# Softmax sums of a windowed attention: two key blocks added on GpSimd, and the ones matmuls moved behind the row's next product

## The chip, the cores and the metric

One NeuronCore of a Trainium2 chip runs the whole program. The metric is the device time of one execution in microseconds.

## The reference

Eight parts run one after the other on 4096 tokens of 128 features: a gated linear recurrence, a two-layer transformer with windowed attention, an attention with ALiBi biases, a mixture of experts, an attention with 8-wide rotated heads, a feed-forward net with ternary weights, a low-rank attention with 32-wide rotation, and a linear layer given in the frequency domain. The change touches the windowed attention alone. It is called for two layers, over 16 rows of 256 tokens, with 8 heads of 64 features:

```python
def local_attention(q, k, v):            # window w = 64 tokens
    bq = q.reshape(b, h, w, WINDOW, d) * QK_SCALE
    ...                                  # each query block looks at its own key block and the one before
    sim = jnp.einsum('bhwid,bhwjd->bhwij', bq, bk)
    mask = (i < j) | (i > j + WINDOW) | (j == -1)
    sim = jnp.where(mask, -jnp.finfo(sim.dtype).max, sim)
    attn = jax.nn.softmax(sim, axis=-1)
    out = jnp.einsum('bhwij,bhwjd->bhwid', attn, bv)
```

The softmax's denominator is, for each query, the sum of its weights over the keys of two blocks (of one block for the first query block).

## The kernel before

`local_attention` (L974) writes a separate program for each engine. `every_row` (L953) walks i over 16 rows plus a tail of 5, and each `step` is cut into four quarters x = 0 to 3. A quarter works on several rows at once: it projects row i (`product`, L1064), transposes row i-1 or i-2 (`columns_of`, L1072), takes scores of row i-2 or i-3 for the maxima (`scores`, L1090), and for row i-4 computes the exponentiated weights (`keyed`, L1104, then ScalarE L1244) and the attention itself (`values`, L1126). The heads come in two groups g; group 0 is attended in quarter 1 and group 1 in quarter 3. The output projection (`output`, L1152) of row i-5 stands in quarter 1. "A full row" below is a step with i from 5 to 15, in which every one of these is alive: 11 in each layer.

The order on each engine is the order of the code. Semaphores tie the engines together, and PSUM banks limit them: bank 0 holds the product, banks 2 and 3 the attention's values (columns 0 to L) and its sums (L to 2L), and bank 1 is used twice in every quarter, once by `columns_of` and once by a second job: project_values (L1144) in quarters 0 and 3, output in 1, shifts (L1158) in 2. `ends` and `bank_read` (L1167 to L1183) make either user wait until the one before was read. So `columns_of` in quarter 2 waits until row i-5's output was added to the residual and stored, which is L1376 on VectorE; in quarters 0, 1 and 3 it waits for a copy by ScalarE.

TensorE's order in quarter 1 is columns_of, values of group 0, output, product; in quarter 3 columns_of, values of group 1, project_values, product. `values` holds, for each of four key blocks j, four 64x64 matmuls with V and four with ones, over 128 query columns (64 for the last block). They read the weights `pr`, laid out by key block: for query block j the weights of its two key blocks stand beside one another, 64 columns each, after the lone first 64 columns.

After the ones matmuls come, per group: on ScalarE the logarithm (`lsum`, L1247) and an exponential (`rec`, L1250), on VectorE `near_one` (L1290, instruction L1294), on ScalarE `left` (L1276), on GpSimd `inv` (L1047), on VectorE `divide` (L1296, instruction L1301), which frees banks 2 and 3. VectorE's order in quarters 1 and 3 is `near_one`, then (quarter 1) L1376, then `rotate` (L1338). In quarter 0 it is `clamped` (L1322), divide of group 1, `maximum`, `inverse_norms` (L1328, its last instruction L1335), `negated` (its last L1320), rotate. GpSimd's order in a quarter is `qn` (L1039), in quarters 1 and 3 `inv`, then `tc` (L1052), and in quarter 2 two shifted copies (L1026, L1028). ScalarE's quarter ends with the square of the product (`sq`, L1272) and `left`.

Of the kernel before, what the change touches and what calls it, by code (L numbers as in the profile page):

```python
# [12 lines left out]
ALU = mybir.AluOpType  # L13
ACT = mybir.ActivationFunctionType
# [5 lines left out]
P = 128  # L20
# [953 lines left out]
def local_attention(k, layer, w, rope, X0, Yd):  # L974
# [7 lines left out]
    with ExitStack() as ctx:  # L982
# [18 lines left out]
        m2 = sb("m2", [P, NB, P])  # L1001
        mT = sb("mt", [P, MSLOTS, NB, P], BF16)
        pr = sb("pr", [P, LA_GROUPS, 2, COLS])
        lsum = sb("lsum", [P, 2, L])
        rec = sb("rec", [P, 2, L])
        two = sb("two", [P, 1])
# [8 lines left out]
        @block.gpsimd  # L1015
        def _(pool):
            nc.gpsimd.memset(m2[:], 0.0).then_inc(s.la_init, 1)
            pool.wait_ge(s.la_init, 3 * layer + 1)
            nc.gpsimd.memset(hs[64:128, :, 0:1], 0.0).then_inc(s.la_init, 1)
            pool.wait_ge(s.la_init, 3 * layer + 2)  # L1020
            nc.gpsimd.memset(two[:], 2.0).then_inc(s.la_init, 1)
            pool.wait_ge(s.la_init, 3 * (layer + 1))

            def shift_in(r):
                n = r % QSLOTS
                nc.gpsimd.tensor_copy(hs[0:64, n, :], X0[0:64, bass.ds(r * L, L)]).then_inc(s.la_shifted, 1)  # L1026
                pool.wait_ge(s.la_shifted, 2 * (row0 + r) + 1)
                nc.gpsimd.tensor_copy(hs[64:128, n, 1:L], X0[64:128, bass.ds(r * L, L - 1)]).then_inc(s.la_shifted, 1)  # L1028
                pool.wait_ge(s.la_shifted, 2 * (row0 + r + 1))
            shift_in(0)  # L1030

            def step(i, n):
                for x in range(4):
                    if live(i, 1):
                        u = 4 * (row0 + i - 1) + x
                        if x == 0:
                            pool.wait_ge(s.la_norm, 3 * (row0 + i))
                        at_least(pool, s.la_qkt, u - 1)
                        nc.gpsimd.tensor_tensor(heads(qn[:, x % 2, :]), heads(tc[:, x, :]),  # L1039
                                                rn[:, x, :].unsqueeze(2).to_broadcast([P, H8, D64]), ALU.mult  # L1040
                                                ).then_inc(s.la_qn, 1)
                        pool.wait_ge(s.la_qn, u + 1)
                    if live(i, 4) and x % 2 == 1:
                        u = LA_GROUPS * (row0 + i - 4) + x // 2
                        pool.wait_ge(s.la_left, u + 1)
                        at_least(pool, s.la_divided, u)
                        nc.gpsimd.tensor_tensor(inv[:], left[:], rec[:], ALU.mult).then_inc(s.la_inv, 1)  # L1047
                        pool.wait_ge(s.la_inv, u + 1)
                    if live(i, 0):
                        u = 4 * (row0 + i) + x  # L1050
                        pool.wait_ge(s.la_rot, u + 1)
                        nc.gpsimd.tensor_tensor(tc[:, x, :], ta[:, x % 2, :], tb[:, x % 2, :], ALU.add).then_inc(s.la_tc, 1)  # L1052
                        pool.wait_ge(s.la_tc, u + 1)
                    if live(i, -1) and x == 2:
                        if live(i, QSLOTS - 1):
                            pool.wait_ge(s.la_vprod, 2 * (row0 + i - QSLOTS + 2))
                        shift_in(i + 1)
            every_row(step, 5, 1)

        @block.tensor  # L1060
        def _(pe):
# [64 lines left out]
            def values(r, g):  # L1126
                u = LA_GROUPS * (row0 + r) + g
                pe.wait_ge(s.la_prob, u + 1)
                if g == 0:
                    pe.wait_ge(s.la_vread, 2 * (row0 + r + 1))  # L1130
                at_least(pe, s.la_divided, u)
                for j in range(NB):
                    lo, n = j * D64, min(2 * D64, L - j * D64)
                    for at, total in ((0, False), (L, True)):
                        for e in range(2):
                            for c in range(2):
                                half = slice(64 * c, 64 * c + 64)
                                one = k.cf("ones", 0, D64)[half, :] if total else V[half, r % VSLOTS, j, 2 * g + e, :]
                                m = nc.tensor.matmul(ps[64 * e:64 * e + 64, 2 + c, at + lo:at + lo + n], one,  # L1139
                                                     pr[half, g, e, 2 * lo:2 * lo + n], start=(j == 0 and not total),  # L1140
                                                     stop=(j == NB - 1 and total), skip_group_check=True)
                m.then_inc(s.la_attended, 1)

            def project_values(r, t):  # L1144
# [40 lines left out]
            def step(i, n):  # L1185
                for x in range(4):
# [27 lines left out]
                    if x == 3 and live(i, 2):  # L1214
                        ends(i, x, 1)
                        project_values(i - 2, 0)
                    if live(i, 0):
                        product(i, x)
            every_row(step, 5, 1)
# [2 lines left out]
        def _(act):  # L1222
# [3 lines left out]
            def step(i, n):  # L1226
                b = row0 + i
                for x in range(4):
# [9 lines left out]
                    if live(i, 4):  # L1238
                        g = x // 2
                        u = LA_GROUPS * (b - 4) + g  # L1240
                        if x % 2 == 0:
                            act.wait_ge(s.la_keyed, u + 1)
                            at_least(act, s.la_attended, u - LA_GROUPS + 1)
                            nc.scalar.activation(pr[:, g, :, :], ps[:, 6:8, 0:COLS], ACT.Exp, scale=8.0).then_inc(s.la_prob, 1)  # L1244
                        else:
                            act.wait_ge(s.la_attended, u + 1)
                            nc.scalar.activation(lsum[:], ps[:, 2:4, L:2 * L], ACT.Ln).then_inc(s.la_logsum, 1)  # L1247
                            act.wait_ge(s.la_logsum, u + 1)
                            at_least(act, s.la_inv, u)
                            nc.scalar.activation(rec[:], lsum[:], ACT.Exp, scale=-1.0).then_inc(s.la_rec, 1)  # L1250
                    if live(i, 1) and x == 0:
                        act.wait_ge(s.la_clamped, b)
                        nc.scalar.activation(lv[:], vc[:], ACT.Ln).then_inc(s.la_ln, 1)
# [9 lines left out]
                    if live(i, 3) and x == 2:  # L1263
                        r = i - 3
                        act.wait_ge(s.la_shift, row0 + r + 1)
                        if r >= MSLOTS:
                            at_least(act, s.la_keyed, LA_GROUPS * (row0 + r - MSLOTS + 1))
                        nc.scalar.copy(mT[:, r % MSLOTS, :, :].rearrange("p j t -> p (j t)"), ps[:, 1, :]).then_inc(s.la_mt, 1)
                    if live(i, 0):
                        act.wait_ge(s.la_product, 4 * b + x + 1)  # L1270
                        at_least(act, s.la_ss, 4 * b + x - 1)
# [1527 lines left out]
class Signals:  # L2799


    def __init__(self, new):
# [76 lines left out]
        self.la_mt = new("la_mt")  # L2879
        self.la_keyed = new("la_keyed")  # L2880
        self.la_prob = new("la_prob")
        self.la_attended = new("la_attended")
        self.la_rec = new("la_rec")
        self.la_divided = new("la_divided")
# [280 lines left out]
```

## Time and profile before

| what | value |
|---|---|
| median of three runs | 2357.25 us (2349.84, 2357.25, 2357.5) |
| the profiled execution, its own time | 2347.32 us |
| its span | 2345.5 us |
| mean granted TensorE clock | 0.911 |
| busy: TensorE matmul, weight load | 1979.4 us (84%), 1257.2 us (54%) |
| busy: VectorE, ScalarE, GpSimd | 1399.5 us (60%), 1167.0 us (50%), 728.0 us (31%) |

The shares are means over the eight parts. The two windowed attentions run from 193 to about 542 us and from 634 to about 982 us. A timeline row tells when an instruction started, how long it took, its engine, line, output and inputs, and in brackets how long its engine had been idle before it and what ended that. TensorE's matmuls overlap one another, so the distance between two starts is its pace, and the printed durations are longer than that.

### The profile page before, as it was taken

Reading aid. Unit: us, or ns where it says so; the run is one execution under the profiler, and the core shown is the slowest. Engines: PE = TensorE matmul, PEld = TensorE weight load, DVE = VectorE, ACT = ScalarE, POOL = GpSimd, SP = SyncE. Lnnn points to the kernel's source line nnn. Section 1 sums busy time; section 2 is a strip of 40 time slices with the busy share of each in tenths; the row PEclk is TensorE's granted clock in tenths of the full one; section 3 lists DMA queues with packets and bytes.
Section 4 is the critical chain, followed back from the end, with each engine's and each line's share of the span. In section 5 each row is a group of like instructions: output and inputs, shape, how many; then the busy total and the mean of one; then the engine's idle time right before and its main releaser. Section 6 shows DMA issues by size and latency. Waiting matters only on the chain. (4 is left out here: it accounts for less than half of the span.)

```text
span 2345.5 us, 68845 instructions
## 1 busy us (share of the span) xinstructions
PE 1979.4 (84%) x28845; PEld 1257.2 (54%) x28845; DVE 1399.5 (60%) x2804; ACT 1167.0 (50%) x1864; POOL 728.0 (31%) x759
## 2 busy tenths in 40 slices
PE   5596999987869999696799989449998958999997
PEld 1242677763337776432555559225555414677765
DVE  5455788834578886355577735557774154556562
ACT  5562566655436666464266644316665441333333
POOL 0213666721057675202332012522220022223230
PEclk8797999998989999997699989769999976899999
DMA  3000000000000000000745511224441003333431
GB/s 136 0 0 1 2 3 3 3 3 0 0 1 3 3 3 3 2 1 6 188 114 120 138 46 41 63 58 99 97 98 40 6 36 114 114 120 120 144 124 37
DMA packets 93704, 122.43 MB, mean 52 GB/s; under 512 B 9376, under 2 KB 80384, under 8 KB 90048
## 3 DMA queue, kind: packets, MB, share of 16 engines
q1 hardware_dynamic: 91352, 113.84, 17.5%
q8 instruction: 232, 3.80, 0.7%
q0 software_dynamic: 2048, 4.20, 0.6%
q14 instruction: 72, 0.59, 0.1%
HBM read 67.62 MB, written 49.15 MB: 50 GB/s over the span
## 5 line engine op out<-in xcount | busy, mean ns | idle before, releaser
L1663 ACT ACTIVATE at_pr<-ps 128x768 f32<-128x768 f32 x256 | 204.0, 811 | 94.0 <-PE ps L1564 85.7
L1052 POOL TENSOR_TENSOR la_tc<-la_ta,la_tb 128x512 f32<-128x512 f32 x128 | 162.6, 1271 | 112.2 <-DVE la_tb L1348 108.1
L1069 PE MATMUL ps<-w_l0f,la_hs 128*128 128x512 f32 x256 | 153.0, 682 | 47.0 <-DVE la_tb L1348 40.8
L1988 ACT ACTIVATE at_pr<-ps 128x640 f32<-128x640 f32 x128 | 90.1, 704 | 187.2 <-PE ps L1891 187.2
L2030 DVE TENSOR_REDUCE at_m<-ps 128x2 f32<-128x512 f32 (+3 forms) x256 | 113.5, 486 | 107.6 <-PE ps L1891 103.2
L1708 DVE TENSOR_REDUCE at_m<-ps 128x2 f32<-128x512 f32 x256 | 174.3, 681 | 0.0
L2281 POOL TENSOR_TENSOR at_parts<-at_ta,at_tb 128x512 f32<-128x512 f32 x64 | 81.2, 1269 | 251.7 <-DVE at_tb L2271 247.7
L1039 POOL TENSOR_TENSOR la_qn<-la_tc,la_rn 128x512 f32<-128x512 f32 x128 | 134.0, 1047 | 52.9 <-issue 36.9
L1707 DVE TENSOR_REDUCE at_m<-ps 128x2 f32<-128x256 f32 x256 | 107.8, 421 | 69.3 <-PE ps L1564 66.5
L1564 PE MATMUL ps<-cast 64*64 64x256 bf16 x2048 | 147.3, 278 | 0.0
L1346 DVE TENSOR_TENSOR la_ta<-ps,la_tab 128x512 f32<-128x512 f32 x128 | 88.2, 689 | 95.2 <-ACT la_sq L1272 95.2
L1272 ACT ACTIVATE la_sq<-ps 128x512 f32<-128x512 f32 x128 | 76.4, 597 | 119.1 <-PE ps L1069 119.1
L1614 PE MATMUL ps<-at_pr,at_v 128*32 128x256 f32 (+1 forms) x2048 | 120.2, 333 | 0.4
L1047 POOL TENSOR_TENSOR la_inv<-la_left,la_rec 128x512 f32<-128x512 f32 x64 | 81.7, 1276 | 113.4 <-ACT la_left L1276 73.2
L1906 PE MATMUL ps<-at_ks,at_qs 40*64 40x256 f32 (+3 forms) x2048 | 108.4, 331 | 8.5 <-DVE at_m L2030 4.5
L1139 PE MATMUL ps<-la_pr,la_v 64*64 64x128 f32 (+1 forms) x2048 | 100.9, 265 | 15.1 <-DVE la_oT L1301 13.6
L1581 PE MATMUL ps<-at_ks,at_qs 54*64 54x128 bf16 (+3 forms) x2048 | 90.7, 254 | 25.4 <-ACT at_pr L1663 13.2
L1076 PEld LDWEIGHTS ps<-conf,la_qn 128*128 128x128 f32 x512 | 61.2, 145 | 86.5 <-issue 40.0
L1924 PE MATMUL ps<-at_qs,at_ks 41*64 41x256 f32 (+3 forms) x2048 | 97.0, 305 | 3.2 <-ACT at_pr L1988 3.2
L1598 PE MATMUL ps<-at_qs,at_ks 56*64 56x256 bf16 (+3 forms) x2048 | 91.9, 256 | 5.5 <-DVE at_m L1708 4.5
L1139 PE MATMUL ps<-la_pr,conf 64*64 64x128 f32 (+1 forms) x2048 | 93.9, 260 | 0.0
L1906 PEld LDWEIGHTS ps<-at_ks,at_qs 40*64 40x64 f32 x2048 | 64.9, 142 | 53.8 <-issue 34.3
(378 smaller groups left out, 4868.5 us busy)
## 6 DMA issues: line engine op xcount, KB each, us to landing
scratch_latent<-at_parts SPq DMA_DIRECT2D x32, 640.0 KB
at_qs<-scratch_latent SPq DMA_DIRECT2D x32, 320.0 KB
at_ks<-scratch_latent SPq DMA_DIRECT2D x32, 320.0 KB
scratch_alibi<-at_parts SPq DMA_DIRECT2D x32, 192.0 KB
at_ks<-scratch_alibi SPq DMA_DIRECT2D x32, 192.0 KB
scratch_rope<-at_parts SPq DMA_DIRECT2D x32, 192.0 KB
at_ks<-scratch_rope SPq DMA_DIRECT2D x32, 192.0 KB
w_l0f<-in_l0f SPq DMA_DIRECT2D x2, 1689.5 KB, 15.5
```

Of the source, the lines that this page charges most:

```text
L1039: nc.gpsimd.tensor_tensor(heads(qn[:, x % 2, :]), heads(tc[:, x, :]), rn[:, x, :].unsqueeze(2).to_broadcast([P, H8, D64]), ALU.mult).then_ ...
L1052: nc.gpsimd.tensor_tensor(tc[:, x, :], ta[:, x % 2, :], tb[:, x % 2, :], ALU.add).then_inc(s.la_tc, 1)
L1069: nc.tensor.matmul(ps[:, 0, :], hs[:, i % QSLOTS, t * P:(t + 1) * P], w("wq" if p < 2 else "wk"), start=True, stop=True).then_inc(s.la_pro ...
L1139: m = nc.tensor.matmul(ps[64 * e:64 * e + 64, 2 + c, at + lo:at + lo + n], one, pr[half, g, e, 2 * lo:2 * lo + n], start=(j == 0 and not t ...
L1564: m = nc.tensor.matmul(out, k.cb("ident", 64 * e, 64)[r, :], rows.unsqueeze(1).to_broadcast([64, 2, P]), start=False, stop=True, skip_grou ...
L1614: m = nc.tensor.matmul(o, V[:, n, q, 4 * half + j, 24 * slot:24 * slot + 32], pr[:, x % RING, e, cols:cols + L - first], start=(q == 0 and ...
L1663: nc.scalar.activation(pr[:, p % RING, :, :], ps[:, at:at + 2, 0:384], ACT.Exp, scale=scale).then_inc(s.at_prob, 1)
L1707: nc.vector.tensor_reduce(m2[:, r, 0, x:16:8], ps[:, at:at + 2, 0:128], AX.X, ALU.max, negate=True)
L1708: nc.vector.tensor_reduce(m2[:, r, 1, x:16:8], ps[:, at:at + 2, 128:384], AX.X, ALU.max, negate=True).then_inc(s.at_max, 1)
L1906: nc.tensor.matmul(ps[64 * c:64 * c + 64, 2 + e, col:col + 64 * (j + 1)], q[:, 64 * j:64 * j + 64], kk[:, 0:64 * (j + 1)], start=(col == 0 ...
L1924: nc.tensor.matmul(ps[64 * c:64 * c + 64, 6 + e, col:col + L - 64 * j], kk[:, 64 * j:64 * j + 64], q[:, 64 * j:L], start=(col == 0), stop= ...
L2030: m = nc.vector.tensor_reduce(m2[:, r, j, x // 2:HP:4], ps[:, 2:4, col:col + 64 * (j + 1)], AX.X, ALU.max, negate=True)
```

## The change

GpSimd gets a new instruction in quarters 0 and 2: once the weights of the group are there, it adds, for query blocks 1 to 3, the weights of the two key blocks, and writes the sum to a new tile `both`. The ones matmuls leave `values`. They form `sums`, which waits for `both`, multiplies the first query block's weights and the three added ones (64 and 192 columns) by ones, and stands in quarters 1 and 3 behind the second bank-1 job and ahead of the product. The semaphore `la_attended` is now raised by `sums`. On ScalarE `lsum` and `rec` move behind the copies of V and mT.

```diff
--- before.py
+++ after.py
@@ -1001,6 +1001,7 @@
         m2 = sb("m2", [P, NB, P])
         mT = sb("mt", [P, MSLOTS, NB, P], BF16)
         pr = sb("pr", [P, LA_GROUPS, 2, COLS])
+        both = sb("both", [P, LA_GROUPS, 2, (NB - 1) * D64])
         lsum = sb("lsum", [P, 2, L])
         rec = sb("rec", [P, 2, L])
         two = sb("two", [P, 1])
@@ -1046,6 +1047,13 @@
                         at_least(pool, s.la_divided, u)
                         nc.gpsimd.tensor_tensor(inv[:], left[:], rec[:], ALU.mult).then_inc(s.la_inv, 1)
                         pool.wait_ge(s.la_inv, u + 1)
+                    if live(i, 4) and x % 2 == 0:
+                        u, g = LA_GROUPS * (row0 + i - 4) + x // 2, x // 2
+                        pool.wait_ge(s.la_prob, u + 1)
+                        twice = pr[:, g, :, D64:COLS].rearrange("p e (j h t) -> p e j h t", h=2, t=D64)
+                        nc.gpsimd.tensor_tensor(both[:, g, :, :].rearrange("p e (j t) -> p e j t", t=D64),
+                                                twice[:, :, :, 0, :], twice[:, :, :, 1, :], ALU.add).then_inc(s.la_summed, 1)
+                        pool.wait_ge(s.la_summed, u + 1)
                     if live(i, 0):
                         u = 4 * (row0 + i) + x
                         pool.wait_ge(s.la_rot, u + 1)
@@ -1131,14 +1139,26 @@
                 at_least(pe, s.la_divided, u)
                 for j in range(NB):
                     lo, n = j * D64, min(2 * D64, L - j * D64)
-                    for at, total in ((0, False), (L, True)):
-                        for e in range(2):
-                            for c in range(2):
-                                half = slice(64 * c, 64 * c + 64)
-                                one = k.cf("ones", 0, D64)[half, :] if total else V[half, r % VSLOTS, j, 2 * g + e, :]
-                                m = nc.tensor.matmul(ps[64 * e:64 * e + 64, 2 + c, at + lo:at + lo + n], one,
-                                                     pr[half, g, e, 2 * lo:2 * lo + n], start=(j == 0 and not total),
-                                                     stop=(j == NB - 1 and total), skip_group_check=True)
+                    for e in range(2):
+                        for c in range(2):
+                            half = slice(64 * c, 64 * c + 64)
+                            nc.tensor.matmul(ps[64 * e:64 * e + 64, 2 + c, lo:lo + n], V[half, r % VSLOTS, j, 2 * g + e, :],
+                                             pr[half, g, e, 2 * lo:2 * lo + n], start=(j == 0), stop=False,
+                                             skip_group_check=True)
+
+            def sums(r, g):
+                u = LA_GROUPS * (row0 + r) + g
+                pe.wait_ge(s.la_summed, u + 1)
+                for e in range(2):
+                    for c in range(2):
+                        half = slice(64 * c, 64 * c + 64)
+                        nc.tensor.matmul(ps[64 * e:64 * e + 64, 2 + c, L:L + D64], k.cf("ones", 0, D64)[half, :],
+                                         pr[half, g, e, 0:D64], start=False, stop=False, skip_group_check=True)
+                for e in range(2):
+                    for c in range(2):
+                        half = slice(64 * c, 64 * c + 64)
+                        m = nc.tensor.matmul(ps[64 * e:64 * e + 64, 2 + c, L + D64:2 * L], k.cf("ones", 0, D64)[half, :],
+                                             both[half, g, e, :], start=False, stop=True, skip_group_check=True)
                 m.then_inc(s.la_attended, 1)
 
             def project_values(r, t):
@@ -1214,6 +1234,8 @@
                     if x == 3 and live(i, 2):
                         ends(i, x, 1)
                         project_values(i - 2, 0)
+                    if x % 2 == 1 and live(i, 4):
+                        sums(i - 4, x // 2)
                     if live(i, 0):
                         product(i, x)
             every_row(step, 5, 1)
@@ -1242,12 +1264,6 @@
                             act.wait_ge(s.la_keyed, u + 1)
                             at_least(act, s.la_attended, u - LA_GROUPS + 1)
                             nc.scalar.activation(pr[:, g, :, :], ps[:, 6:8, 0:COLS], ACT.Exp, scale=8.0).then_inc(s.la_prob, 1)
-                        else:
-                            act.wait_ge(s.la_attended, u + 1)
-                            nc.scalar.activation(lsum[:], ps[:, 2:4, L:2 * L], ACT.Ln).then_inc(s.la_logsum, 1)
-                            act.wait_ge(s.la_logsum, u + 1)
-                            at_least(act, s.la_inv, u)
-                            nc.scalar.activation(rec[:], lsum[:], ACT.Exp, scale=-1.0).then_inc(s.la_rec, 1)
                     if live(i, 1) and x == 0:
                         act.wait_ge(s.la_clamped, b)
                         nc.scalar.activation(lv[:], vc[:], ACT.Ln).then_inc(s.la_ln, 1)
@@ -1266,6 +1282,13 @@
                         if r >= MSLOTS:
                             at_least(act, s.la_keyed, LA_GROUPS * (row0 + r - MSLOTS + 1))
                         nc.scalar.copy(mT[:, r % MSLOTS, :, :].rearrange("p j t -> p (j t)"), ps[:, 1, :]).then_inc(s.la_mt, 1)
+                    if live(i, 4) and x % 2 == 1:
+                        u = LA_GROUPS * (b - 4) + x // 2
+                        act.wait_ge(s.la_attended, u + 1)
+                        nc.scalar.activation(lsum[:], ps[:, 2:4, L:2 * L], ACT.Ln).then_inc(s.la_logsum, 1)
+                        act.wait_ge(s.la_logsum, u + 1)
+                        at_least(act, s.la_inv, u)
+                        nc.scalar.activation(rec[:], lsum[:], ACT.Exp, scale=-1.0).then_inc(s.la_rec, 1)
                     if live(i, 0):
                         act.wait_ge(s.la_product, 4 * b + x + 1)
                         at_least(act, s.la_ss, 4 * b + x - 1)
@@ -2879,6 +2902,7 @@
         self.la_mt = new("la_mt")
         self.la_keyed = new("la_keyed")
         self.la_prob = new("la_prob")
+        self.la_summed = new("la_summed")
         self.la_attended = new("la_attended")
         self.la_rec = new("la_rec")
         self.la_divided = new("la_divided")
```

## Rows read from the trace of the kernel before

**Rows 1.** The page's second part: TensorE's granted clock in 40 slices of the span.

```profile
PEclk8797999998989999997699989769999976899999
```

**Rows 2.** Stretches: length; busy PE, PEld, DVE, ACT, POOL (instructions); clock; DMA share, GB/s.

```profile
193.00:270.00 77.00, 54.15 (x526) 28.60 (x530) 50.99 (x110) 27.93 (x53) 43.66 (x44) 0.76 0.00 1
270.00:455.00 185.00, 184.99 (x3629) 133.32 (x3624) 148.67 (x324) 121.85 (x215) 129.07 (x124) 1.00 0.01 3
...
480.00:520.00 40.00, 33.35 (x856) 26.43 (x855) 13.84 (x28) 20.75 (x33) 8.47 (x7) 1.00 0.01 3
...
710.00:895.00 185.00, 184.99 (x3627) 133.35 (x3622) 148.76 (x325) 121.72 (x215) 128.96 (x124) 1.00 0.01 3
```

**Rows 3.** Timeline of TensorE over one full row: start, duration in us, then the instructions.

```profile
398.55 1.12 PE L1069 MATMUL ps<-w_l0f,la_hs 128*128 128x512 f32 x2
399.51 0.60 PE L1076 MATMUL ps<-conf,la_qn 128*128 128x128 f32 x4
...
404.83 0.45 PE L1139 MATMUL ps<-la_pr,la_v 64*64 64x128 f32 x8
405.10 0.40 PE L1139 MATMUL ps<-la_pr,conf 64*64 64x128 f32 x8
405.32 0.40 PE L1139 MATMUL ps<-la_pr,la_v 64*64 64x128 f32 x8
...
406.53 1.99 PE L1155 MATMUL ps<-la_oT,w_l0f 128*128 128x256 f32 x8
408.36 1.02 PE L1069 MATMUL ps<-w_l0f,la_hs 128*128 128x512 f32 x2
409.22 0.60 PE L1076 MATMUL ps<-conf,la_qn 128*128 128x128 f32 x4
...
416.66 1.13 PE L1069 MATMUL ps<-w_l0f,la_hs 128*128 128x512 f32 x2
```

**Rows 4.** Timeline of the vector engine, and of TensorE's weight loads, same row.

```profile
407.96 0.69 DVE L1294 TENSOR_TENSOR la_near<-ps,la_rec 128x512 f32<-128x512 f32 x1 [0.17 <-ACT la_rec L1250]
408.57 0.42 DVE L1376 TENSOR_TENSOR y<-ps,xn 128x256 f32<-128x256 f32 x1
...
409.04 0.54 PEld L1076 LDWEIGHTS ps<-conf,la_qn 128*128 128x128 f32 x4 [0.49 <-DVE y L1376]
```

**Rows 5.** Timeline of the scalar engine, same row.

```profile
403.45 0.58 ACT L1261 COPY la_v<-ps 128x512 f32<-128x512 f32 x1 [0.43 <-PE ps L1148]
...
406.67 0.60 ACT L1247 ACTIVATE la_lsum<-ps 128x512 f32<-128x512 f32 x1 [1.09 <-PE ps L1139]
407.30 0.63 ACT L1250 ACTIVATE la_rec<-la_lsum 128x512 f32<-128x512 f32 x1
```

**Rows 6.** Timeline of GpSimd, same row: four instructions around its idle time.

```profile
404.85 1.06 POOL L1039 TENSOR_TENSOR la_qn<-la_tc,la_rn 128x512 f32<-128x512 f32 x1 [1.17 <-issue]
407.35 1.28 POOL L1052 TENSOR_TENSOR la_tc<-la_ta,la_tb 128x512 f32<-128x512 f32 x1 [1.44 <-DVE la_tb L1348]
...
413.46 1.04 POOL L1039 TENSOR_TENSOR la_qn<-la_tc,la_rn 128x512 f32<-128x512 f32 x1
415.71 1.28 POOL L1052 TENSOR_TENSOR la_tc<-la_ta,la_tb 128x512 f32<-128x512 f32 x1 [1.21 <-DVE la_tb L1348]
```

**Rows 7.** Timeline of three engines in the first layer's tail, from one attention to the next.

```profile
495.33 0.45 PE L1139 MATMUL ps<-la_pr,la_v 64*64 64x128 f32 x8
...
502.19 0.45 PE L1139 MATMUL ps<-la_pr,la_v 64*64 64x128 f32 x8 [0.30 <-DVE la_oT L1301]
...
498.46 0.69 DVE L1294 TENSOR_TENSOR la_near<-ps,la_rec 128x512 f32<-128x512 f32 x1 [3.73 <-ACT la_rec L1250]
...
500.04 1.28 POOL L1047 TENSOR_TENSOR la_inv<-la_left,la_rec 128x512 f32<-128x512 f32 x1 [7.60 <-ACT la_left L1276]
```

**Rows 8.** Two lines of the vector engine: duration in ns, min/median/max.

```profile
L1320 DVE TENSOR_TENSOR la_m<-la_nm,la_nb x32: 169/1024/1028, 243.7 to 950.4; 128x16 f32<-128x16 f32 x32
...
L1326 DVE TENSOR_SCALAR la_vc<-la_ss x32: 181/182/1180, 210.4 to 914.9; 128x32 f32<-128x32 f32 x32
```

## Prediction

> **What bounds the kernel now.** I read the page first for where the two windowed attentions lie: slices of 58.6 us, and a granted clock of 0.9 to 1.0 in most of those that hold them [rows 1]. The stretches come next [rows 2]. In the full rows of both layers TensorE is busy 184.99 of 185.00 us at a granted clock of 1.00 (2.4 GHz); VectorE, ScalarE and GpSimd are busy 149, 122 and 129 us. TensorE is the bound there, by its own work and not by a wait. In the first rows and in the tail (33.35 of 40 us busy) it waits for others.
>
> The timeline shows the pattern [rows 3]. A full row repeats every 18.11 us (product at 398.55, the next row's at 416.66). Between a product and the transposes behind it lie 0.86 us (408.36 to 409.22), the product's own pace: the reader of bank 1 is hidden behind it. In quarter 1 the cover is just enough: the residual add L1376 starts at 408.57, takes 0.42 us, and the transposes' weight load at 409.04 was released by it [rows 4]. That add is the place to watch, since on VectorE it stands behind `near`, and `near` waits for ScalarE's two steps on the sums.
>
> **The change, part by part.**
>
> *Ones matmuls removed.* `values` runs from 404.83 to 406.53 [rows 3], 1.70 us for eight blocks, of which one of 128 columns paces at 0.22 us (405.10 to 405.32). The ones had 128+128+128+64 columns, 0.76 us; the V part alone keeps 0.95 us. `sums` has 64+192 columns, in 64-column units of 0.11 us some 0.43 us. Saved per group 0.32 us, per full row 0.64 us. These matmuls are on the path, so this counts in full, until something else is late.
>
> *The add on GpSimd.* 128x384 elements from two SBUF inputs. The nearest row is the 512-element add L1052 at 1.28 us [rows 6]; by elements 0.96 us. Lower bound 0.8 (the multiplication with a broadcast, 1.04 us for 512, scaled), upper bound 1.3, should the strided runs cost as much as 512 elements. I take 1.0. Its inputs are there when GpSimd gets to it. It falls into the idle 1.44 us before `tc` in quarter 0 and the 1.21 us in quarter 2 [rows 6]: hidden, and done shortly before `sums` needs it, with only some 0.1 us to spare in quarter 1 (below). Without that cover it would delay `sums` by what it is late.
>
> *The move of the sums.* In quarter 1 the order becomes columns_of, V part, output, sums, product. Call the end of `sums` T. Product starts at T and covers 0.86 us. From T the chain is: `lsum` starts T+0.14 (406.67 against 406.53), `rec` 0.63 later, `near` 0.66 after `rec` (407.30 to 407.96), L1376 0.61 after `near`, and the transposes 0.65 after L1376 (408.57 to 409.22) [rows 3 to 5]. Together 2.69 us. Before, the same chain began at 406.53, 1.83 us of output ahead of the product, and ended in time. Now output's result waits in bank 1 behind a softmax step that has nothing to do with it. Stall: 2.69 - 0.86 = 1.83 us in every full row. Behind the waiting `near` stand L1376 and `rotate`; TensorE, which waits for L1376, has keyed, scores, shifts and the next product queued behind columns_of. Rotate is late by about 0.4 us, and a product waits only for the rotation before it, which is done by then.
>
> *ScalarE's new order.* The copies of V no longer wait for `lsum` and `rec`. Behind quarter 3's product this removes the 0.10 us by which the transposes lag (399.51 - 398.55 - 0.86) [rows 3]: -0.10. In exchange `near`, `left` and everything behind them come about 0.5 us later against the product: ScalarE's queue in quarter 0 had 0.43 us idle before its V copy [rows 5], which absorbs most; I add 0.2 us (bounds 0 and 0.5). The copy of mT isn't touched by it, since quarter 2 has no `lsum`.
>
> Per full row: 1.83 - 0.64 - 0.10 + 0.20 = +1.29 us, 18.11 to 19.40. Eleven rows per layer: +14.2.
>
> *The tail.* There the path is a chain from one attention to the next: 495.33 to 502.19, 6.86 us, of which `near` to `inv` is 1.58 (498.46 to 500.04) [rows 7]. It starts when the ones end. In quarter 1 the ones now end 0.95+1.83+0.43 = 3.21 us after `values` begins and not 1.70: +1.51, four times (i from 16 to 19). In quarter 3 of i = 17 project_values lies between: 0.95+1.02+0.43 - 1.70 = +0.7; in that of 16 the V copy is free earlier, -0.9; in the last two there is no bank-1 job, -0.32 each. Sum +5.2. The first rows change by 0.1. A layer costs 14.2 + 5.2 = 19.4 us, both layers +39.
>
> *The port that VectorE and GpSimd share.* L1320, sixteen elements from two SBUF inputs, takes 169 ns when GpSimd is idle and 1024 ns as a median, running beside `qn`; L1326, with one SBUF input, takes 181 ns at the least and 1180 ns at the most [rows 8]. So they do get held up by GpSimd. With `both` directly behind `qn`, L1320 could be held for 2 us in place of 1; rotate of quarter 0 would then end about 1 us later, but the 1.83 us stall follows and takes most of it: 0 to 0.1 us per row, I take 0. L1326 is worse placed: `inv` now starts about 0.5 us later against it, so that it asks while `inv` runs. Served between `inv` and `tc` it costs 0.1 us, which lies in my 0.2; held until `tc` ends, it is a rival below.
>
> The Trainium skill, "SBUF — State Buffer", section "Who interferes with whom", says that a VectorE instruction with two SBUF inputs, or in a two-port mode, and a GpSimd instruction that reads SBUF exclude each other for the whole instruction, whoever starts first. By that rule, the trace agrees for L1320 (1024 against 169 ns); it doesn't say who wins when one waits and the other has the next instruction queued, and that is what decides the rival.
>
> *Clock.* Nothing suggests a change of level: the tail, 83% busy, was granted 1.00, and only the start, 70% busy, fell to 0.76 [rows 2]. The new full rows leave TensorE idle 1.8 of 19.4 us. Cost 0.
>
> **Sum.** The profiled execution's own time was 2347.3 us, so 2347.3 + 39 = 2386. The median of the three runs shown stands 9.9 us above that execution, the lowest 2.5 us above; a new median should lie between 2386 and 2396. I say 2391, that is 39 above a present 2352.
>
> **Rivals.**
>
> *A, the forecast:* the residual add waits behind `near`, +39: 2391. For it: it follows from the order of the code and from five distances of one timeline. Chance 0.66.
>
> *B, GpSimd's sum comes late as well.* Place: L1326 in quarter 0 held until `tc` ends, 1.3 us (like its 1180 ns). Through ScalarE's `lv` and `y1`, `inverse_norms` and `qn` of quarter 0 it makes `both` late by that, and `sums` of quarter 1 with it. By my working `both` ends some 0.1 us before `sums` is reached, so nearly all counts: 1.3 x 22 = +29, together 2420. A slower add (1.3 us) is a small form of it: +0.3 x 22 = +7. For it: the maximum of rows 8. Against it: in full rows L1326 kept its 182 ns between `inv` and `tc`, that is, in just such a gap. Chance 0.18.
>
> *C, no difference that can be measured.* About 0.5%, 12 us, is what a measurement of this kernel can tell from no change. The stall would have to be below 1.2 us a row and the tail's chain half of what I reckon, for instance if ScalarE and VectorE overlapped more than their start distances show. It gives 2340 to 2364, most likely 2358. Chance 0.09.
>
> *D, faster.* The mechanism: bank 1 isn't what TensorE waits for in quarter 2, because L1376 is served early enough, and the saved ones count. Place: the transposes behind the product of quarter 1. Price: -0.64 - 0.10 per full row, x 22 = -16, with the tail's +10 or without it: 2336 to 2346. It decides from a chain shorter than 0.86 + 0.74 = 1.60 us from T to the transposes; I count 2.69. For it is only that VectorE has room to be early (149 of 185 us busy); against it that `near` is ahead in the queue. That the change doesn't do what it says (the matmuls are not fewer) I rule out from the diff. Chance 0.07.
>
> **Numbers.** Slower by over 0.5%: A and B, 0.84, and a little of C, 0.85. Within: 0.08. Faster: 0.07. The range must leave out no more than 2 in 10. Above, it takes B with some margin below its worst, 2422; below, it takes A with the bounds of its terms: the V copy at 0 in place of 0.2 (-4), the stall 0.3 us shorter (-7), no growth of the tail (-10), gives 2370. C and D lie below and are left out, 0.16.
>
> **What the profile of the changed kernel would show.** Right: a full row of 19.4 us; in quarter 2 the weight load of the transposes idle for about 1.8 us, released by L1376, 22 times; TensorE about 91% busy in the full rows; L1376 directly behind `near` and both about 1.5 us after the sums; 512 ones matmuls of 64 columns and 512 of 192 in place of 2048. The add on GpSimd at 0.9 to 1.1 us, started right behind `qn`. In the tail, 8.4 us from the group-0 attention to the group-1 attention. B would show `sums` waiting for `both`, and L1326 at over 1 us in full rows. The prediction is wrong if the transposes of quarter 2 follow the product at 0.86 us, or if a full row is at or below 18.1 us.

## The result, and the profile after

| | before | changed |
|---|---|---|
| median of four runs, us | 2357.38 (2349.84 to 2362.63) | 2408.22 (2407.25 to 2411.96) |
| span of the profiled execution, us | 2345.5 | 2410.2 |
| first layer's attention, start of the first copy to start of the last residual add | 193.1 to 541.4 | 194.0 to 571.5 |
| second layer's | 634.5 to 981.0 | 662.9 to 1039.0 |

The change makes the kernel slower: ratio 1.0239, 95% interval 1.0213 to 1.0264. Of the 64.7 us between the two spans, 29.2 lie in the first layer's attention and 29.6 in the second's; the other 5.9 lie in parts that weren't touched. The length of those parts differs by as much without any change: in the ten traces kept, before and after and of the experiments, what lies outside the two attentions takes between 1642 and 1657 us. So the effect of an edit is read below from the attentions in the traces, beside the ratios.

TensorE over one full row of the changed kernel, the same view as [rows 3]:

```profile
406.05 1.02 PE L1077 MATMUL ps<-w_l0f,la_hs 128*128 128x512 f32 x2
...
407.47 1.00 PE L1145 MATMUL ps<-la_pr,la_v 64*64 64x128 f32 x32
408.40 1.08 PE L1168 MATMUL ps<-w_l0f,la_hs 128*64 128x256 f32 x8
409.41 0.34 PE L1155 MATMUL ps<-la_pr,conf 64*64 64x64 f32 x8
409.58 0.51 PE L1160 MATMUL ps<-la_both,conf 64*64 64x192 f32 x8
410.02 1.12 PE L1077 MATMUL ps<-w_l0f,la_hs 128*128 128x512 f32 x2
...
414.80 1.12 PE L1077 MATMUL ps<-w_l0f,la_hs 128*128 128x512 f32 x2
...
416.30 1.00 PE L1145 MATMUL ps<-la_pr,la_v 64*64 64x128 f32 x32
417.23 1.99 PE L1175 MATMUL ps<-la_oT,w_l0f 128*128 128x256 f32 x8
419.15 0.34 PE L1155 MATMUL ps<-la_pr,conf 64*64 64x64 f32 x8
419.31 0.51 PE L1160 MATMUL ps<-la_both,conf 64*64 64x192 f32 x8
419.75 1.12 PE L1077 MATMUL ps<-w_l0f,la_hs 128*128 128x512 f32 x2
422.25 0.66 PE L1084 MATMUL ps<-conf,la_qn 128*128 128x128 f32 x4 [1.38 <-DVE y L1399]
```

L1077 is the product: the row runs from 406.05 to 425.61, 19.56 us against 18.11. The window begins with quarter 3. Quarters 3, 0, 1 and 2, from product to product, take 3.97, 4.78, 4.95 and 5.86 us, against 4.14, 4.79, 5.02 and 4.16. All of the loss is in quarter 2, where the transposes L1084 begin 2.50 us after the product and not 0.86. What they wait for stands in VectorE's and ScalarE's timelines of the same moment, which answer to [rows 4, 5]; the third is the weight load of the sums:

```profile
421.18 0.69 DVE L1317 TENSOR_TENSOR la_near<-ps,la_rec 128x512 f32<-128x512 f32 x1 [1.46 <-ACT la_rec L1291]
421.79 0.41 DVE L1399 TENSOR_TENSOR y<-ps,xn 128x256 f32<-128x256 f32 x1
```

```profile
419.89 0.60 ACT L1288 ACTIVATE la_lsum<-ps 128x512 f32<-128x512 f32 x1 [2.85 <-PE ps L1160]
420.52 0.63 ACT L1291 ACTIVATE la_rec<-la_lsum 128x512 f32<-128x512 f32 x1
```

```profile
419.15 0.21 PEld L1155 LDWEIGHTS ps<-la_pr,conf 64*64 64x64 f32 x8 [0.33 <-POOL la_both L1054]
```

TensorE does its jobs in order, so the output projection stood ahead of the sums, which began at 419.15; its residual add starts at 421.79, directly behind `near`. The lines that wait for L1399, over the whole execution (us in total, times):

```profile
  PEld ps L1084: 44.1, 20
  PE ps L1084: 27.6, 20
```

There are 22 full rows; in the first of each layer the trace names GpSimd's `qn` instead, with 1.54 us. GpSimd's new add and the instruction of VectorE that the second rival was about (L1349, before L1326 [rows 8]), min/median/max in ns:

```profile
L1054 POOL TENSOR_TENSOR la_both<-la_pr x64: 990/997/1003, 262.6 to 1027.6; 128x384 f32<-128x384 f32 x64
...
L1349 DVE TENSOR_SCALAR la_vc<-la_ss x32: 310/317/1173, 211.4 to 959.7; 128x32 f32<-128x32 f32 x32
```

Last, the tail of the first layer, from the last product on, against 70.90 us at a granted clock of 0.94 before (columns as in [rows 2]), and four stretches of it:

```profile
488.30:572.00 83.70, 57.42 (x1102) 43.06 (x1098) 24.29 (x50) 32.78 (x53) 26.30 (x24) 0.84 0.01 2
...
515.00:523.80 8.80, 6.52 (x151) 5.18 (x149) 2.77 (x8) 3.81 (x6) 2.01 (x2) 1.00 0.01 2
523.80:530.00 6.20, 6.16 (x144) 4.64 (x144) 1.58 (x3) 1.81 (x3) 0.25 (x1) 0.72 0.01 3
...
533.00:538.00 5.00, 4.90 (x56) 3.72 (x60) 1.45 (x5) 0.00 (x0) 0.30 (x1) 0.66 0.01 3
...
549.00:556.00 7.00, 6.17 (x72) 5.02 (x76) 0.69 (x1) 0.17 (x1) 0.99 (x1) 0.58 0.01 2
```

From the last product to the last residual add, the tail grew by 12.8 us in the first layer (83.2 against 70.4) and by 13.4 in the second (83.3 against 69.9), and TensorE ran parts of it near its lower level of 1.2 GHz. It first did so near the tail's start, behind a wait like that of the full rows: there too the transposes come behind a residual add (499.93) that stood behind `near`. The job after them (L1121) then takes 1.55 us to the next one, for 0.82 in the kernel before.

```profile
500.55 1.09 PE L1084 MATMUL ps<-conf,la_qn 128*128 128x128 f32 x4 [2.59 <-issue]
501.57 1.77 PE L1121 MATMUL ps<-la_qk 64*64 64x128 f32 x32
```

### The profile page after: what moved, and what is told of

It is laid out like the page before. It is cut to its first block and busy times, and to the rows that moved or that the text cites. A ratio compares the mean times of both kernels' runs of the same rounds, so it can differ in the third digit from the quotient of the medians.

```text
span 2410.2 us, 66925 instructions
## 1 busy us (share of the span) xinstructions
PE 1994.3 (83%) x27821; PEld 1236.3 (51%) x27821; DVE 1400.6 (58%) x2804; ACT 1168.1 (48%) x1864; POOL 791.0 (33%) x823
## 5 line engine op out<-in xcount | busy, mean ns | idle before, releaser
L1077 PE MATMUL ps<-w_l0f,la_hs 128*128 128x512 f32 x256 | 154.8, 689 | 45.5 <-DVE la_tb L1371 39.3
L1060 POOL TENSOR_TENSOR la_tc<-la_ta,la_tb 128x512 f32<-128x512 f32 x128 | 162.6, 1270 | 84.1 <-DVE la_tb L1371 79.8
L1317 DVE TENSOR_TENSOR la_near<-ps,la_rec 128x512 f32<-128x512 f32 x64 | 44.2, 691 | 148.8 <-ACT la_rec L1291 148.8
L1084 PEld LDWEIGHTS ps<-conf,la_qn 128*128 128x128 f32 x512 | 62.1, 146 | 123.1 <-issue 55.3
L1084 PE MATMUL ps<-conf,la_qn 128*128 128x128 f32 x512 | 83.3, 288 | 42.8 <-DVE y L1399 27.6
L1288 ACT ACTIVATE la_lsum<-ps 128x512 f32<-128x512 f32 x64 | 38.2, 597 | 119.5 <-PE ps L1160 118.4
```

Source lines behind the costliest of these rows:

```text
L1077: nc.tensor.matmul(ps[:, 0, :], hs[:, i % QSLOTS, t * P:(t + 1) * P], w("wq" if p < 2 else "wk"), start=True, stop=True).then_inc(s.la_pro ...
L1084: m = nc.tensor.transpose(ps[:, 1, c * P:(c + 1) * P], qn[:, p % 2, c * P:(c + 1) * P], k.cf("identf"))
```

## The experiments

All are edits of the changed kernel. Ratios are to the kernel before, run on the same chip: its median is 2349.2 us for the first three experiments and for "A better place for both", and 2352.3 us for the others.

**Is it the residual add's place in VectorE's queue?**

```diff
-                    if x % 2 == 1 and live(i, 4):
-                        near_one(i - 4, x // 2)
                     if live(i, 5) and x == 1:
                         dve.wait_ge(s.la_out, b - 4)
                         ...
+                    if x % 2 == 1 and live(i, 4):
+                        near_one(i - 4, x // 2)
```

> The changed kernel with one edit on VectorE: in quarter 1 the residual add L1399 stands ahead of near and no longer behind it. Bank theory (the transposes of quarter 2 wait for a residual add queued behind near): quarter 2 falls from 5.86 us back to about 4.2, a full row from 19.56 to 17.9, so 22 rows give back some 36 us; the tails stay long (they are a chain through the sums, not through bank 1). Time about 2372, that is 10 to 20 us above the kernel before. Rival (GpSimd's new add, by its own time or the port it shares with VectorE, is what costs): the row stays above 19 us and the time within 10 us of the changed kernel's 2408.

Measured: 2368.8 us, ratio 1.0074 (1.0047 to 1.0102). A full row:

```profile
397.00 1.02 PE L1077 MATMUL ps<-w_l0f,la_hs 128*128 128x512 f32 x2
...
400.62 0.34 PE L1155 MATMUL ps<-la_pr,conf 64*64 64x64 f32 x8 [0.18 <-POOL la_both L1054]
...
410.96 1.12 PE L1077 MATMUL ps<-w_l0f,la_hs 128*128 128x512 f32 x2
411.93 0.60 PE L1084 MATMUL ps<-conf,la_qn 128*128 128x128 f32 x4
...
415.23 1.02 PE L1077 MATMUL ps<-w_l0f,la_hs 128*128 128x512 f32 x2
```

Quarter 2 is back at 4.27 us and its transposes follow the product after 0.97 us. The row is 18.23 us, not 17.9: quarter 3 now takes 4.23 us for 3.97, since its sums wait for GpSimd (idle 0.18 us), and quarter 2 is 0.07 above the 4.2 expected. The bank theory holds; the edit touches nothing of GpSimd, so the rival falls. The tails were expected to stay, and did so only in part: 78.3 and 78.1 us, for 83.2 and 83.3. Their first quarter 1 has the same queue, and from its attention to the next one is 8.94 us with the edit and 12.50 without it (9.28 in the kernel before).

**Does the add on GpSimd pay?** `sums` multiplies all of `pr` by ones again, and the add is gone:

```diff
-                pe.wait_ge(s.la_summed, u + 1)
 ...
-                nc.tensor.matmul(ps[..., L:L + D64], k.cf("ones", 0, D64)[half, :], pr[half, g, e, 0:D64], ...)
 ...
-                nc.tensor.matmul(ps[..., L + D64:2 * L], k.cf("ones", 0, D64)[half, :], both[half, g, e, :], ...)
+                for j in range(NB):
+                    ...
+                    nc.tensor.matmul(ps[..., L + lo:L + lo + n], k.cf("ones", 0, D64)[half, :], pr[half, g, e, 2 * lo:2 * lo + n], ...)
```

> The changed kernel without GpSimd's add: the ones multiply all of the weights again (128+128+128+64 columns), but at the late place, ahead of the product. Bank theory: the stall of quarter 2 stays; the late ones take 0.93 us in place of 0.61, twice a row, less the 0.09 us that they waited for the add in quarter 1: a row of 20.1 us, time about 13 us above the changed kernel, 2421. Rival (the add on GpSimd costs): faster than the changed kernel by 10 us or more.

Measured: 2432.5 us, ratio 1.0356 (1.0321 to 1.0392).

```profile
389.58 1.02 PE L1070 MATMUL ps<-w_l0f,la_hs 128*128 128x512 f32 x2
...
403.01 1.00 PE L1148 MATMUL ps<-la_pr,conf 64*64 64x128 f32 x32
403.94 1.13 PE L1070 MATMUL ps<-w_l0f,la_hs 128*128 128x512 f32 x2
406.45 0.66 PE L1077 MATMUL ps<-conf,la_qn 128*128 128x128 f32 x4 [1.38 <-DVE y L1388]
...
409.81 1.02 PE L1070 MATMUL ps<-w_l0f,la_hs 128*128 128x512 f32 x2
```

The row is 20.23 us and keeps its stall of 1.38 us: the stall needs no GpSimd. The add itself saves 0.67 us a row at this place. The first half of the change was good; the second, the move alone, costs 2.12 us a row (20.23 against 18.11). The time is 11 us above what was expected. By the traces the two attentions are 22 us longer than the changed kernel's: 15 in the full rows, 4.5 in the tails, the rest elsewhere in them.

The run also settles a doubt about the add. I had read the 0.33 us by which the weight load of the sums is idle in quarter 1 as a wait for GpSimd, since the trace names `both`. Here no add exists, and it is idle as long:

```profile
403.01 0.86 PEld L1148 LDWEIGHTS ps<-la_pr,conf 64*64 64x64 f32 x32 [0.33 <-issue]
```

From the output projection to the sums it is 1.92 us in both kernels (403.01 - 401.09 and 419.15 - 417.23). So the add doesn't delay the sums in a full row of the changed kernel, the rival (that it costs) falls, and the 0.09 us that I subtracted for it was not there to save.

**Is the tail's growth the order too?** In steps without a product, `sums` directly behind `values`, and `lsum` and `rec` at their former place:

```diff
                     if x == 1 and live(i, 4):
                         values(i - 4, 0)
+                        if not live(i, 0):
+                            sums(i - 4, 0)
 ...
-                    if x % 2 == 1 and live(i, 4):
+                    if x % 2 == 1 and live(i, 0) and live(i, 4):
                         sums(i - 4, x // 2)
```

> The changed kernel with the sums (and ScalarE's two steps on them) put back directly behind the V part in the tail steps alone, those without a product. If the tail's growth (70.4 to 83.2 us in the first layer, granted clock 0.94 to 0.84) comes from output and project_values standing ahead of the sums in the chain, the tail falls back to 67 to 70 us with a granted clock of 0.93 or more, and the time is 24 to 30 us below the changed kernel, about 2381; full rows stay at 19.56 us. Rival (the tail is longer because the clock fell for another reason, or because GpSimd's add stands in its chain): the tail stays above 78 us.

Measured: 2383.8 us, ratio 1.0173 (1.0126 to 1.0220). The tail from its last product:

```profile
489.30:561.00 71.70, 52.77 (x1102) 39.30 (x1098) 24.50 (x50) 33.24 (x53) 26.37 (x24) 0.89 0.01 2
```

From the last product to the last residual add it is 71.2 us (489.31 to 560.5), a little above what was expected, at a clock of 0.89, below the 0.93 expected. Twelve of the 12.8 us are gone, and 12.5 of the second layer's 13.4. What stays in the way is the tail's first quarter 1, where the early sums do wait for GpSimd's add, and the jobs behind them run slow:

```profile
498.25 0.49 PE L1155 MATMUL ps<-la_pr,conf 64*64 64x64 f32 x8 [1.79 <-POOL la_both L1054]
```

From that attention to the next it is 12.49 us, as in the changed kernel; of the six steps behind it four are down to 6.5 us. So the add stands in the chain in this one step, as the rival had it, and the order makes the rest. The full rows are unchanged at 19.56 us. Against the changed kernel the time fell by 13 to 16 us by the ratios (1.0228 and 1.0239), less than the 24 to 30 expected, and the runs of this kernel spread from 2379.7 to 2406.7. By the traces the two attentions are 25 us shorter.

**Do the two make up the whole?** Both repairs, the first only where there is a product.

> Both repairs in one kernel: the residual add ahead of near where there is a product, and the sums directly behind the V part where there is none. If the stall on the residual add and the tail's chain are the whole cost of the change, their removal adds up: a full row of 18.23 us as with the first repair alone (0.12 us above the kernel before, 22 rows: +3), tails of 71 us as with the second (+1 each): 0 to 8 us above the kernel before. Rival (something else costs as well, such as GpSimd's load): 15 us or more above it.

Measured: 2354.3 us, ratio 1.0015 (0.9996 to 1.0033), row 18.21 us. With the stall and the tail's order taken away nothing is left that the times can tell; by the traces the two attentions stay 5.4 us longer than in the kernel before. The control, the changed kernel on that chip:

> The changed kernel itself, on the same chip as the other three, as their control. Both theories: a ratio of 1.021 to 1.026 to the kernel before, as in its first measurement.

Measured: 2401.8 us, ratio 1.0228 (1.0199 to 1.0257).

**How much room has the add on GpSimd?** The same add twice, into the same tile:

```diff
+                        for again in range(2):
-                        nc.gpsimd.tensor_tensor(both[:, g, :, :]...).then_inc(s.la_summed, 1)
-                        pool.wait_ge(s.la_summed, u + 1)
+                            nc.gpsimd.tensor_tensor(both[:, g, :, :]...).then_inc(s.la_summed, 1)
+                            pool.wait_ge(s.la_summed, 2 * u + 1 + again)
 ... (sums)
-                pe.wait_ge(s.la_summed, u + 1)
+                pe.wait_ge(s.la_summed, 2 * u + 2)
```

> The changed kernel with GpSimd's add done twice in a row, into the same tile. Theory: the add has no slack left in quarter 1, where the sums already wait for it (weight loads idle 0.33 us), and some 1.4 us of slack in quarter 3: a row longer by 1.1 us (up to 1.4 if tc and rotate are pushed too), 22 rows: 24 to 31 us above the changed kernel. Rival (the add is hidden, as the prediction costed it): within 5 us of the changed kernel.

Measured: 2436.4 us, ratio 1.0368 (1.0342 to 1.0395), 35 us above the control and 4 us above the range expected.

```profile
406.36 1.99 PE L1176 MATMUL ps<-la_oT,w_l0f 128*128 128x256 f32 x8
409.19 0.34 PE L1156 MATMUL ps<-la_pr,conf 64*64 64x64 f32 x8 [0.83 <-POOL la_both L1055]
```

The row is 20.47 us, 0.91 more: in quarter 1 almost all of another microsecond reaches TensorE, in quarter 3 nothing (3.97 us as before). The two adds together take 2.07 us and the one took 1.00, so of 1.07 us more 0.91 came through: in quarter 1 the add had some 0.16 us to spare. The two attentions are 31 us longer than the control's, of which 20 are full rows and 3 the tails; the other 8 lie in the rest of the attentions.

**A better place for both.** GpSimd adds ahead of `qn`, and the sums follow the V part everywhere, ScalarE as before:

```diff
 (GpSimd)
+                    if live(i, 4) and x % 2 == 0:
+                        ... both = twice[..., 0, :] + twice[..., 1, :] ...
                     if live(i, 1):
                         ... qn ...
-                    if live(i, 4) and x % 2 == 0:
-                        ... both ...
 (TensorE)
                         values(i - 4, 0)
+                        sums(i - 4, 0)
 ...
-                    if x % 2 == 1 and live(i, 4):
-                        sums(i - 4, x // 2)
```

> GpSimd's add kept, but ahead of qn in quarters 0 and 2, and the sums directly behind the V part in every step, with ScalarE's order as before. If the add itself is nearly free and the place of the sums is what costs: no stall of 1.4 us on L1399, the sums save 0.32 us a group since they follow 64-column tiles without a change of tile shape, a row of about 17.5 us, tails shorter by 2 to 3 us each: time 12 to 20 us below the kernel before, about 2340. Rival (the add's load on GpSimd and the port makes qn, tc or rotate late): a row at or above 18.1 us and the time at or above the kernel before.

Measured: 2342.4 us, ratio 0.9975 (0.9954 to 0.9995). Less than expected. TensorE, then VectorE:

```profile
405.53 1.00 PE L1145 MATMUL ps<-la_pr,la_v 64*64 64x128 f32 x32
406.35 0.29 PE L1155 MATMUL ps<-la_pr,conf 64*64 64x64 f32 x8
406.47 0.51 PE L1160 MATMUL ps<-la_both,conf 64*64 64x192 f32 x8
406.91 1.99 PE L1175 MATMUL ps<-la_oT,w_l0f 128*128 128x256 f32 x8
408.75 1.13 PE L1077 MATMUL ps<-w_l0f,la_hs 128*128 128x512 f32 x2
410.27 0.66 PE L1084 MATMUL ps<-conf,la_qn 128*128 128x128 f32 x4 [0.40 <-DVE y L1399]
```

```profile
404.99 0.77 DVE L1356 TENSOR_TENSOR la_y<-la_y 128x32 f32<-128x32 f32 x1
...
408.62 0.67 DVE L1375 TENSOR_REDUCE la_ss<-la_sq 128x8 f32<-128x512 f32 x1
409.21 0.67 DVE L1317 TENSOR_TENSOR la_near<-ps,la_rec 128x512 f32<-128x512 f32 x1
409.81 0.41 DVE L1399 TENSOR_TENSOR y<-ps,xn 128x256 f32<-128x256 f32 x1
```

V part and sums take 1.38 us, 0.32 less than the 1.70 of [rows 3]: the full saving. But the row is 18.20 us, since quarter 2 takes 4.88. VectorE is busy from `ss` into `near` without a gap and comes to the residual add 0.6 us too late. It is late by itself now: L1356, 182 ns in the kernel before (there L1333), takes 770 ns, beside GpSimd's add (404.71 to 405.71). The trace suggests that the port has a part in the lateness; no run here takes it away by itself, so how large it is stays open. The next run keeps this edit and gives the residual add its place ahead of `near`, in steps with a product.

> The kernel with GpSimd's add ahead of qn and the sums directly behind the V part, which had a row of 18.20 us, its quarter 2 still 4.88 us since near held back the residual add for 0.6 us; here the residual add stands ahead of near in steps with a product. Bank theory: quarter 2 falls to 4.2 us, a row to about 17.5 us, 22 rows give back some 15 us against that kernel: 18 to 24 us below the kernel before, ratio 0.990 to 0.993. Rival (VectorE, held up by GpSimd at the shared port, is late with whatever stands first): quarter 2 stays above 4.6 us and the time within 5 us of that kernel.

Measured: 2326.9 us (2325.1 to 2338.0), ratio 0.9914 (0.9889 to 0.9938): faster than both kernels, by 0.9% against the one before.

```profile
400.20 1.13 PE L1077 MATMUL ps<-w_l0f,la_hs 128*128 128x512 f32 x2
...
404.94 1.12 PE L1077 MATMUL ps<-w_l0f,la_hs 128*128 128x512 f32 x2
405.90 0.62 PE L1084 MATMUL ps<-conf,la_qn 128*128 128x128 f32 x4
...
409.22 1.02 PE L1077 MATMUL ps<-w_l0f,la_hs 128*128 128x512 f32 x2
```

```profile
405.40 0.41 DVE L1399 TENSOR_TENSOR y<-ps,xn 128x256 f32<-128x256 f32 x1
405.73 0.68 DVE L1317 TENSOR_TENSOR la_near<-ps,la_rec 128x512 f32<-128x512 f32 x1
```

Quarter 2 takes 4.28 us and a row 17.62 (product to product over four quarters, 391.60 to 409.22), 0.49 below the kernel before: 11 us over 22 rows. The tails are 2.7 and 1.3 us shorter, and the two attentions together 15.8 us. The ratio says 20 us and the medians 25; what is above 15.8 lies in parts that weren't touched. L1356 still takes 767 ns here (401.17), so the rival, that VectorE is late with whatever stands first, falls: the residual add starts 0.46 us behind the product.

## Why the prediction was right, step by step

The direction, the range, and the mechanism of the full rows held. The forecast for the median was 2391 and it was 2408; in the traces the attentions cost 58.8 us, not 39. Of the 20 us that are missing, 16 are the tails, and 3.5 the full rows. That 2408 still lies in the range is in part luck: its upper end, 2422, was set to take in rival B, which didn't come, and not a slow clock in the tails, which did.

- **The stall in quarter 2** was foreseen in place, cause and count. Its size was 2.50 - 0.86 = 1.64 us a row and not 1.83: the residual add starts 2.04 us behind the product, as summed, but I had taken 0.65 us from its start to the transposes from a row where the product was still running; free of that they follow after 0.46.
- **Ones matmuls removed.** The V part took 0.93 us, as reckoned. The `sums` took 0.60 (419.15 to 419.75) and 0.61 (409.41 to 410.02), not 0.43. This was the mis-sized term in the row: the saving was 0.16 us a group, not 0.32. Where the same matmuls follow the V part, the two take 1.38 us together, which is 0.45 on top of the 0.93, and the saving is 0.32. So some 0.16 us goes with the place, between two jobs of other tile shapes; the trace shows the weight loads of the sums idle for 0.39 us on "issue" in quarter 3 (409.41), for 0.28 to 0.39 elsewhere at such a change. That the change of shape itself is the reason is argued, not shown.
- **The add on GpSimd** took 997 ns, for 1.0 taken, and was hidden in the full rows. The sums begin 1.92 us after the output projection, where the product had begun after 1.83, but they do so without any add as well. That only some 0.1 us was to spare in quarter 1 was foreseen; doubling the add gives 0.16.
- **ScalarE's new order.** Neither the -0.10 us nor the +0.20 came. The transposes follow quarter 3's product after 0.96 us (410.02 to 410.98), exactly as before (398.55 to 399.51), though the copy of V no longer holds them: the weight load that waited for it before now shows "issue". So the 0.10 us was no wait for that copy, a misreading of [rows 3]. Quarter 0 takes 4.78 us, for 4.79 before. What makes the 0.10 is open.
- **Together** +1.45 us a row for +1.29: the stall 0.19 smaller, the saving 0.31 smaller, -0.10 and +0.20 both absent, and 0.15 that no term had (output to sums +0.09; transposes of quarter 2 to the next product 3.36 us for 3.30). So the sum came close partly because its errors cancelled. Over 22 rows 31.9 us for 28.
- **The tail** was the term that failed: +5.2 us a layer was forecast, and +12.8 and +13.4 were measured. The chain is the one described; in the step where the clock stayed at 1.00 it grew from 6.86 to 8.60 us (515.25 to 523.85), for 8.4 forecast. But I took the clock at no cost, since the former tail had 1.00 up to 520 us. The table shows the first layer's tail from one attention to the next, with what the prediction's terms say of each step, and the stretches in which its jobs ran slow, with the granted clock:

| step | before | after | grew by | forecast | slow stretch in it |
|---|---|---|---|---|---|
| i = 16, group 0 to group 1 | 9.28 | 12.50 | 3.22 | 1.51 | 500.5 to 504.0: 0.55 |
| to i = 17, group 0 | 8.88 | 8.32 | -0.56 | -0.9 | none |
| i = 17, group 0 to group 1 | 6.86 | 8.60 | 1.74 | 1.51 | none |
| to i = 18, group 0 | 6.85 | 9.25 | 2.40 | 0.7 | 523.8 to 530.0: 0.72 |
| i = 18, group 0 to group 1 | 6.84 | 10.23 | 3.39 | 1.51 | 533.0 to 538.0: 0.66 |
| to i = 19, group 0 | 6.83 | 6.50 | -0.33 | -0.32 | 543.0 to 549.0: 0.92 |
| i = 19, group 0 to group 1 | 8.07 | 11.01 | 2.94 | 1.51 | 549.0 to 556.0: 0.58 |
| to the last output projection | 6.83 | 6.91 | 0.08 | -0.32 | only its last matmuls |

  The four steps with a stretch at 0.55 to 0.72 make 6.7 of the 7.6 us by which the tail exceeds its forecast; each of the others is within 0.4 us of its term. In these four the same jobs took longer: the output projection 3.38 us (534.03 to 537.41) and 3.57 (551.53 to 555.10), for 1.92 at full clock. The former tail had the lower clock only in its last 20 us, at 0.79; its last projection took 3.75 us, as it does here. What brings the lower clock is not shown. In the first two of the four it came after longer waits than before (2.59 us ahead of 500.55 for 0.67, 1.85 ahead of 523.85 for 0.30), but the jobs at 543.33 and 560.84 came after waits of 1.86 and 3.91 us and began at full speed. The run with the sums early in the tail, whose waits are short again but for its first step, had 0.89 and 71.2 us.
- **Rival B** fell: L1349 takes 317 ns and not 1180 in full rows. It asks while `inv` runs and is served at its end, ahead of `tc` (L1349 ends at 414.34, `tc` starts at 414.38). L1343, before L1320, stayed at 1024 ns with the add queued directly behind `qn`: the waiting VectorE instruction got its turn between two of GpSimd's both times.
- **Rival D** would have needed a chain below 1.60 us from sums to transposes; it is 2.50. **Rival C** needed a stall below 1.2 us and a tail's growth of half the forecast; the stall is 1.64 and the growth more than double.

## What to carry to other kernels

When a semaphore or a sum is moved "behind" a job to be out of the way, look at what its readers have queued behind them: here a residual add with its data long ready stood behind `near` on VectorE, and it held the one PSUM bank that TensorE needed next. Halving the work and moving it are two changes; tried one at a time, the first was worth 0.67 us a row and the second cost 2.12. In a tail where the engines wait in turn, each added link counts in full, and with longer waits TensorE may run parts of it at a lower clock: here at 0.55 to 0.72. When a trace names who ended a wait, a run without that instruction tells whether it was the cause: here the weight load idled 0.33 us with GpSimd's add and without it.

## What the runs showed of the hardware

- The same V part and sums take TensorE 1.38 us when one follows the other, and 0.93 + 0.61 = 1.54 us when a projection stands between them.
- Two VectorE instructions of 32 and 16 elements show the port shared with GpSimd: L1356 with two SBUF inputs 182 ns alone and 770 beside the add, which is to say until the add ended; L1343 1024 ns beside `qn`. The Trainium skill, "SBUF — State Buffer", section "Who interferes with whom", says that one of the two holds the port for its whole instruction while the other waits; these rows agree. L1349 has one SBUF input and went from 182 to 317 ns beside `inv`. When GpSimd had another instruction queued, VectorE's waiting one came first in the full rows here (317 and 1024 ns, above).
- GpSimd's add of 384 elements read in runs of 64 takes 997 ns, 512 contiguous ones 1270. By elements that would be 953 (1270 x 384/512), so reading in runs cost 44 ns more than the count of elements says, or less, if a part of the 1270 doesn't shrink with the elements.
